# Gated attention with a routed mixture of experts: the up projections turned round, with the weights as the stationary operand

## What is computed

```python
scores = softmax(xf @ Wg.T); w, idx = top_k(scores, 2); w = w / w.sum(-1)
h1 = _lora_in(xf, W1, b1, A1, B1)      # xf @ W1.T + low-rank part + b1
h3 = _lora_in(xf, W3, b3, A3, B3)
g  = silu(h1) * h3
y_e = _lora_out(g, W2, b2, A2, B2)
y  = einsum('te,ted->td', gates, y_e)
x  = x + tanh(g_ffn[0]) * y
```

## Time and profile before

| | us |
|---|---|
| median of 2 runs | 328.74 (328.02 to 329.46) |
| the profiled execution | 328.63 |
| its span in the trace | 326.8 |
| PE busy | 300.9 (92%) |
| DVE busy | 248.6 (76%) |
| POOL busy | 210.5 (64%) |
| ACT busy | 207.0 (63%) |
| mean granted clock of PE | 0.976 of full speed |

### The profile page before, as it was taken

One profiled execution on the slowest core, in us unless ns is written; L12 is line 12 of the kernel. 1 busy time (PEld: TensorE's weight loads), 2 busy tenths in 40 slices (PEclk: granted clock), 3 DMA queues, 4 the chain that ended last, 5 costly groups with the idle time before them and its releaser, 6 DMA issues. The chain is left out here.

```text
span 326.8 us, 7436 instructions
## 1 busy us (share of the span) xinstructions
PE 300.9 (92%) x1755; PEld 231.7 (71%) x1755; DVE 248.6 (76%) x607; ACT 207.0 (63%) x486; POOL 210.5 (64%) x246
## 2 busy tenths in 40 slices
PE   8669989989999698999999999999999999999992
PEld 4548778777887555876777667677777777777761
DVE  2678879878899988787998877577777777786771
ACT  5625756656679648769657657475675575576562
POOL 2447878967986169776474756466567767676344
PEclk9979999997999969999999999999999999999998
DMA  7957998999884248676665667576553233433300
GB/s 254 391 153 217 283 256 275 279 264 261 262 235 131 67 143 274 203 213 196 154 192 149 189 157 211 132 204 203 138 135 52 49 56 59 67 48 47 50 0 0
DMA packets 30424, 54.35 MB, mean 166 GB/s; under 512 B 7232, under 2 KB 15808, under 8 KB 30112
## 3 DMA queue, kind: packets, MB, share of 16 engines
q1 hardware_dynamic: 14672, 36.10, 34.7%
q0 software_dynamic: 7488, 9.36, 16.8%
q10 hardware_dynamic: 8224, 8.42, 8.3%
HBM read 41.92 MB, written 10.65 MB: 161 GB/s over the span
## 5 line engine op out<-in xcount | busy, mean ns | idle before, releaser
L1079 POOL DMA_INDIRECT out<-ys,cols x39 | 63.5, 1629 | 54.7 <-DMA out<-ys,cols 42.2
L883 ACT ACTIVATE gh<-bank 128x512 fp32r<-128x512 f32 x39 | 23.4, 599 | 54.6 <-PE bank L648 54.4
L640 PE MATMUL bank<-WH,xh 128*128 x156 | 55.8, 439 | 0.0
L1056 POOL DMA_INDIRECT xg<-xn_rows,colg x39 | 41.2, 1056 | 20.5 <-POOL colg L1034 10.3
L992 POOL TENSOR_TENSOR WL<-stage,WH 128x512 bf16<-128x512 f32 x38 | 48.0, 1282 | 8.2 <-ACT WH L752 8.1
L640 PE MATMUL bank<-WH,xl 128*128 x156 | 49.0, 395 | 0.0
L640 PE MATMUL bank<-WL,xb 128*128 x156 | 47.2, 384 | 0.0
L752 ACT ACTIVATE WH<-stage 128x512 fp32r<-128x512 f32 x38 | 22.9, 628 | 18.2 <-DVE stage L1112 14.9
L640 PEld LDWEIGHTS bank<-WH,xl 128*128 128x128 f32 x156 | 29.2, 188 | 6.8 <-DVE xl L1495 0.4
L657 PE MATMUL bank<-WH,gh 128*128 x156 | 32.1, 327 | 1.4 <-ACT gh L883 1.4
L1499 DVE TENSOR_TENSOR gl<-bank,gh 128x512 fp32r<-128x512 f32 x39 | 26.9, 688 | 7.9 <-ACT gh L883 7.4
(11 more groups left out here) (229 smaller groups left out, 711.7 us busy)
## 6 DMA issues: line engine op xcount, KB each, us to landing
BB<-biases_in SPq DMA_DIRECT2D x16, 640.0 KB, 4.0
stage<-w_all_in SPq DMA_DIRECT2D x38, 256.0 KB, 4.5
BA<-biases_in SPq DMA_DIRECT2D x8, 640.0 KB, 4.0
WL<-w_all_in SPq DMA_DIRECT2D x10, 256.0 KB, 4.5
LS<-WH SPq DMA_DIRECT2D x45, 48.0 KB
xn_rows<-xn ACTq DMA_DIRECT2D x8, 256.0 KB, 4.7
out<-x ACTq DMA_DIRECT2D x7, 256.0 KB, 2.5
cx<-ctxT_in ACTq DMA_DIRECT2D x6, 256.0 KB, 6.1
```

The lines of the kernel that those rows point to most:

```text
L640: last = nc.tensor.matmul(dst[:, :], lhs[p][:, c * P:(c + 1) * P], W[:, bass.ds(e * (UNITS * UC) + (2 * kind + c) * UC, HID)], start=(part ...
L883: nc.scalar.activation(gh[:], pG[:, :], ACT.Copy).then_inc(s_gh, 1)
L1056: nc.gpsimd.indirect_dma_start(out=xg[q][:], out_offset=None, in_=xn2_d[0:JA * P, :] if i < NA else xn2_d, in_offset=bass.IndirectOffsetOn ...
L1079: nc.gpsimd.indirect_dma_start(out=out_rows, out_offset=bass.IndirectOffsetOnAxis(ap=cols[:, i:i + 1], axis=0), in_=ys[p][:], in_offset=No ...
```

## The change

In `up` the operands change places. Now a 128x128 block of the weights is stationary and the 128 tokens move, so `pH1` and `pH3` hold the hidden width on the partitions, in four chunks of 128 columns of tokens. A chunk takes two bfloat16 products (`WL` by `xb`) and four float32r ones (the weights' high part by `xh` and by `xl`, for two halves of the width): 24 matmuls of 128 columns for a kind where there were 6 of 512. `g` comes out as `down` wants it, so `g_transposes` and the bank `pG` go, and ACT and DVE make `gh` and `gl` from `g` in SBUF.

The stationary float32r block has a fixed address: before a tile's kind is multiplied, SP copies that kind's 1024 columns of `WH` (128 x 1024 x 4 bytes, 512 KB) inside SBUF into one of the buffers `wk` (three, later four), two copies for each tile. `xh` and `xl` lie in one tensor `xx`. b1 and b3 become columns of the partitions: eight small loads bring them in as 64 rows of 128, PE transposes them once and ACT keeps them in `b13`; DVE adds them spread over the tokens. Only b2 is still spread over the partitions (`b2`, 128 KB for each tile). ACT's `gb` moves ahead of the parts of x.

```diff
-        xh = [sb(tiles, f"xh{p}", [P, D], F32R) for p in range(2)]
-        xl = [sb(tiles, f"xl{p}", [P, D], F32R) for p in range(2)]
-        xb = [sb(tiles, f"xb{p}", [P, D], BF16) for p in range(2)]
+        xx = [sb(tiles, f"xx{p}", [P, CH, 2, P], F32R) for p in range(2)]
+        xb = [sb(tiles, f"xb{p}", [P, CH, P], BF16) for p in range(2)]
...
+        def wk_slot(n):
+            return n % 3 if n < WFOUR else (n - WFOUR + 3) % 4
...
+            def load_bias_rows():
+                sp.wait_ge(s_qT, 2 * B)
+                for e in range(E):
+                    sp.dma_start(brow[e * BCH:(e + 1) * BCH, :], biases[e, 0:2 * HID].rearrange("(c p) -> c p", p=P)
+                                 ).then_inc(s_brow, 16)
+            def load_tile(i, kind, e):
+                n = 2 * i + kind
...
+                if wk_user(n) is not None:
+                    sp.wait_ge((s_h1, s_h3)[wk_user(n) % 2], wk_user(n) // 2 + 1)
+                sp.dma_start(wk[wk_slot(n)][:].bitcast(F32), WH[:, bass.ds(e * (UNITS * UC) + 2 * kind * UC, WCOL)].bitcast(F32)
+                             ).then_inc(s_wk[wk_slot(n)], 16)
...
+            load_bias_rows()
+            for i in range(NT_SLOTS):
+                e = expert_of(i)
+                load_tile(i, 0, e)
+                if i == 1:
+                    load_weights(E - 1, 1, 1)
+                load_tile(i, 1, e)
+                if i == 0:
+                    sp.wait_ge(s_x2, B)
+                    sp.dma_start(out_rows[(B - 1) * S:B * S, 0:D].rearrange("(t p) d -> p t d", p=P), x2[:]).then_inc(s_last, 16)
+                load_scaled(i, e)
+                if i == 1:
+                    load_units(E - 1, 1, 2)
...
+            pe.wait_ge(s_brow, 16 * E)
+            nc.tensor.transpose(pT[:, 0:E * BCH], brow, ident[0:E * BCH, 0:E * BCH]).then_inc(s_bT, 1)
             attend(B, v[1])
...
                 pos_wait(pe, s_h1b if kind == 0 else s_h3b, i)
-                for part, (lhs, W, ready) in enumerate(((xh, WH, s_xh), (xl, WH, s_xl), (xb, WL, s_xb))):
-                    if kind == 0:
-                        pe.wait_ge(ready, i + 1)
+                r = wk_slot(2 * i + kind)
+                for hc in range(HC):
+                    cols = dst[:, hc * P:(hc + 1) * P]
+                    at = lambda c: bass.ds(e * (UNITS * UC) + (2 * kind + c) * UC + hc * P, P)
...
                     for c in range(CH):
-                        last = nc.tensor.matmul(dst[:, :], lhs[p][:, c * P:(c + 1) * P],
-                                                W[:, bass.ds(e * (UNITS * UC) + (2 * kind + c) * UC, HID)],
-                                                start=(part == 0 and c == 0), stop=(part == 2 and c == CH - 1))
+                        nc.tensor.matmul(cols, WL[:, at(c)], xb[p][:, c, :], start=(c == 0), stop=False)
...
+                    if hc == 0:
+                        pe.wait_ge(s_wk[r], wk_loads(2 * i + kind))
+                    for c in range(CH):
+                        for part in range(2):
+                            last = nc.tensor.matmul(cols, wk[r][:, c * HID + hc * P:c * HID + (hc + 1) * P], xx[p][:, c, part, :],
+                                                    start=False, stop=(c == CH - 1 and part == 1))
                 last.then_inc(sig, 1)
-
-            def g_transposes(i):
-                pe.wait_ge(s_g, i + 1)
-                for c in range(HC):
-                    last = nc.tensor.transpose(pG[:, c * P:(c + 1) * P], g[:, c * P:(c + 1) * P], ident[:])
-                last.then_inc(s_gT, 1)
...
             def g_high(i):
-                act.wait_ge(s_gT, i + 1)
+                act.wait_ge(s_g, i + 1)
                 pos_wait(act, s_y, i)
-                nc.scalar.activation(gh[:], pG[:, :], ACT.Copy).then_inc(s_gh, 1)
+                nc.scalar.activation(gh[:], g[:], ACT.Copy).then_inc(s_gh, 1)
```

More of the change, by code:

```diff
@@ L69 @@
 BCOL = 2 * HID + D
+BCH = 2 * HC
+WFOUR = 9
+BRING = 3
 C_TRI, C_IOTA, C_SEG = 0, P, 2 * P
@@ L181, in flamingo @@
         colg = sb(tiles, "colg", [P, NT_SLOTS], U32); cols = sb(tiles, "cols", [P, NT_SLOTS], U32)
-        eid = sb(tiles, "eid", [1, NT_SLOTS], I32); vid = sb(tiles, "vid", [1, NT_SLOTS], I32); bid = sb(tiles, "bid", [1, NT_SLOTS], I32)
+        eid = sb(tiles, "eid", [1, NT_SLOTS], I32); vid = sb(tiles, "vid", [1, NT_SLOTS], I32)
         gsel = sb(tiles, "gsel", [P, 2 + XBUF])
@@ L200, in flamingo @@
         ys = [sb(tiles, f"ys{p}", [P, D]) for p in range(2)]
[L201 to L207, removed]
+        wk = [sb(tiles, f"wk{r}", [P, WCOL], F32R) for r in range(2)]
+        gidxA = sb(tiles, "gidxA", [P, NV], I32); sidxA = sb(tiles, "sidxA", [P, NV], U32)
+        is1A = sb(tiles, "is1A", [P, NV]); is0A = sb(tiles, "is0A", [P, NV])
+        valA = sb(tiles, "valA", [P, NV])
+        b13 = sb(tiles, "b13", [P, E, BCH])
+        wk.append(sb(tiles, "wk2", [P, WCOL], F32R))
+        b2 = [sb(tiles, f"b2_{r}", [P, D]) for r in range(BRING)]
+        wk.append(sb(tiles, "wk3", [P, WCOL], F32R))
         tiles.close()
+        brow = ys[1][0:E * BCH, 0:P]
         gidxB, sidxB = cst[:, C_TRI:C_TRI + NV].bitcast(I32), cst[:, C_TRI + NV:C_TRI + 2 * NV].bitcast(U32)
@@ L234, in flamingo @@
         s_r = sem("s_r")
-        s_bb, s_ba = [sem(f"s_bb{r}") for r in range(BRING)], [sem(f"s_ba{x}") for x in range(E)]
+        s_brow, s_bT, s_b13 = sem("s_brow"), sem("s_bT"), sem("s_b13")
+        s_b2, s_wk = [sem(f"s_b2_{r}") for r in range(BRING)], [sem(f"s_wk{r}") for r in range(4)]
         s_h1b, s_h3b, s_b2g = sem("s_h1b"), sem("s_h3b"), sem("s_b2g")
@@ L291, in ls_of, with wk_loads, wk_user @@
             return kind, (s - 1) * KINDS + kind + 1
-        def bias_loads(i):
-            return 16 * BSLOT[:i + 1].count(BSLOT[i])
+        def wk_slot(n):
+            return n % 3 if n < WFOUR else (n - WFOUR + 3) % 4
+        def wk_loads(n):
+            return 16 * sum(wk_slot(m) == wk_slot(n) for m in range(n + 1))
+        def wk_user(n):
+            return max((m for m in range(n) if wk_slot(m) == wk_slot(n)), default=None)
         def settle(eng):
@@ L436, in load_biases @@
[L436 to L440, removed]
+                    sp.wait_ge(s_last, 16)
+                if i == SAFE and kind == 0:
+                    sp.wait_ge(s_wh, (E - 1) * UNITS + 4)
+                if wk_user(n) is not None:
+                    sp.wait_ge((s_h1, s_h3)[wk_user(n) % 2], wk_user(n) // 2 + 1)
@@ new lines, in load_tile, with load_scaled @@
+                sp.dma_start(wk[wk_slot(n)][:].bitcast(F32), WH[:, bass.ds(e * (UNITS * UC) + 2 * kind * UC, WCOL)].bitcast(F32)
+                             ).then_inc(s_wk[wk_slot(n)], 16)
+            def load_scaled(i, e):
+                r = i % BRING
+                if i == 0:
+                    sp.wait_ge(s_x2, B)
+                if i == 1:
+                    sp.wait_ge(s_xn2, B)
+                    sp.wait_ge(s_last, 16)
+                if i >= BRING:
+                    sp.wait_ge(s_b2g, i - BRING + 1)
+                sp.dma_start(b2[r][:], biases[bass.ds(e, 1), 2 * HID:BCOL].to_broadcast([P, D])).then_inc(s_b2[r], 16)
@@ L618, in _ @@
             keep_clock(5, WL, pS)
-            pX, pH1, pH3, pG, pY = bank[0], bank[1], bank[2], bank[3], bank[4]
+            pX, pH1, pH3, pY = bank[0], bank[1], bank[2], bank[4]
             def x_transposes(i, q):
@@ L675, in tile @@
                 up(pH1, i, p, expert(q), 0, s_h1)
-                if not first:
-                    g_transposes(i - 1)
                 if more:
@@ L869, in _ @@
             first_two(B - 2)
-            pX, pH1, pG = bank[0], bank[1], bank[3]
+            pXc = bank[0][:, 0:D].rearrange("p (c t) -> p c t", c=CH)
             def x_parts(i, p):
@@ L938, in tile @@
                 first_gate(i, q, v)
-                if not first:
-                    g_short(i - 1)
                 if i == 2:
@@ L977, in _ @@
             x_parts(0, 0)
+            act.wait_ge(s_bT, 1)
+            nc.scalar.activation(b13[:].rearrange("p e c -> p (e c)"), pT[:, 0:E * BCH], ACT.Copy).then_inc(s_b13, 1)
             deviation(B - 1)
@@ L1487, in beside_h3 @@
                     row_kinds(2, valB[:], gidxB, gofB[:], nhB[:], sidxB, is0B, is1B)
-            pX, pH1, pH3, pG, pY = bank[0], bank[1], bank[2], bank[3], bank[4]
+            pX, pH1, pH3, pY = bank[0], bank[1], bank[2], bank[4]
+            by_chunk = lambda t: t.rearrange("p (c t) -> p c t", t=P)
             def x_rest(i, p):
@@ L1520, in tile @@
                 p = q % 2
-                x = dve.value_load(bid[0:1, i:i + 1], min_val=0, max_val=E - 1) if i >= NA else 0
+                x = dve.value_load(eid[0:1, i:i + 1], min_val=0, max_val=E - 1)
                 beside_h1(i)
-                pos_wait(dve, s_g, i)
-                if i < NA:
-                    dve.wait_ge(s_bb[BSLOT[i]], bias_loads(i))
-                elif i < NA + E:
-                    dve.wait_ge(s_ba[i - NA], 16)
+                if first:
```

(6 more changed lines are left out.)

93 lines of the change are left out of this document (37 added, 56 removed).

## The result

| | before | after |
|---|---|---|
| median, us | 328.74 (2 runs) | 376.63 (2 runs, 376.61 to 376.66) |
| ratio, 95% interval | | 1.146 (1.138 to 1.154) |
| span in the trace | 326.8 | 374.8 |
| mean granted clock of PE | 0.976 | 0.980 |

A forecast was written before the change was run, and what follows sets the result against it. PE's instructions were taken to bound the tile loop. From 326.8 us, +65.5 for 39 longer tiles, -3 for waits and -0.7 at the end gave 388.6 of span, +1.8 around it: 390 us, range 375 to 418.

The forecast's parts named there:

- The bound: Tile loop: PE's instructions set a tile's cost, pitch 4.84 us late; longer PE work is paid 39 times.
- The price of a product: `up` products of 128 columns: float32r 0.115 us, bfloat16 0.075, set by block loads; a chunk 0.61.
- The sum for a tile: PE's tile: `up` 4.88 us replaces 2.76, transposes of g save 0.44; pitch 6.52, +65.5 us over 39 tiles.
- What lies around it: Early tiles' waits swallowed by longer tiles, -3 us; end of the last tile, -0.7 us.
- The copies: Weight copies inside SBUF: with other traffic 5.31 us of all DMA engines per tile, costing nothing under PE's 6.5.
- the floor under PE: Tile loop: DMA engines' busy time would limit a tile to 5.3 us should PE be quicker.
- A: `up`: float32r loads cheaper behind 128 columns, 0.085 us instead of 0.115; time 353; chance 0.07.
- B: `up`: float32r load and moving do not overlap, 0.163 us a product; +60, time 450; chance 0.07.
- C: `up`: narrow float32r products need as many passes as plain float32, 0.216 us each; +126, time 516; chance 0.11.
- D: PE's clock falls because the array moves columns for only some 60% of a tile; 455 if lasting; chance 0.08.
- E: Copies inside SBUF run at half the loads' rate: 8.6 us a tile, DMA-bound, time 472; chance 0.05.
- F: Not slower: array keeps a block for the next product using it; time 345, or about 317; chance 0.02.

## Why the prediction was right, point by point

**The bound.** Right. PE is busy for 100.00 of 100.00 us after the change and the other engines wait for it. The two runs on columns and block show that it is the float32 loads that fill most of it.

**The price of a product.** The mechanism was right, the sizes a little high. The float32r product was taken at 0.115, and its loads stand 0.111 apart. The two bfloat16 ones were taken at 0.150 and what is left of a chunk is 0.133; among themselves they cost 0.056 (a chunk of six takes 0.33 to 0.34 in the run with all products bfloat16), and the rest is the change of type, which the forecast did not have. A chunk was forecast at 0.61 and is 0.577. The 0.213 for a product of 512 columns was misread, which the sum does not feel:

```profile
250.37 0.62 PE L640 MATMUL bank<-WH,xl 128*128 x2
250.84 0.60 PE L640 MATMUL bank<-WL,xb 128*128 x2
251.28 0.60 PE L648 MATMUL bank<-ident,g 128*128 128x128 f32 x4
```

A float32r product is (250.84 - 250.37) / 2 = 0.235, a bfloat16 one 0.22. The 1.28 for h3 runs between two starts of float32r products that are both shown before their blocks can be there, the second by more; from the start of the second `xh` load to that of the second `gh` load it is 1.38.

**The sum for a tile.** 6.52 forecast, 6.29 measured: 0.28 less for the two kinds; the transposes of x take 0.24 and not 0.13, which the earlier trace rows understated because a float32r product's start is shown while it still waits for the transpose before it; `down` takes 1.45 and not 1.51. The 0.23 are 9 of the 13 us by which the forecast was high. That is the mis-sized term. Of the rest, the first product of tile 0 starts at 119.55 and not at 122.08, 2.5 us, which I can't put down to a part of the change and which is less than the spread of the first `gh` product over the runs. The stated range is a little narrower than its own terms: they add up to 372 and 422.

**What lies around it.** Right in size: the first 24 tiles have 2.9 us over the later pitch, 3.5 expected. At the end, from the last tile but one's `gb` to the last tile's `gh`, 366.02 to 367.84, it is 1.8 us where it was 2.5 (317.04 to 319.54), the forecast 0.7 less.

**The copies.** Right that they are covered, shown by leaving them out (376.5 against 376.6); PE waited 0.5 us for them in all, the start included. Their cost to the DMA engines was overstated, 0.75 x 6.28 = 4.7 us for a tile and not 5.3. But the floor under PE is not the engines' busy time, as I had written: with less work for PE and all copies the tiles lengthen through late scatters and gathers at shares of 0.84 to 0.91, to mean pitches of 5.1 to 5.5 where PE needed 4.4 to 5.0.

**The rivals.** A (0.085 for a float32r product) is out, the same block twice in a row saves nothing. B (0.163) is out. C (four passes for narrow products) is out: with 64 columns in place of 128 the loads still stand 0.111 apart. D: the clock stays at 1.00 through the loop although the array moves columns for 63% of the tile (9472 x 0.417 ns in 6.29). E: a copy of 512 KB lands after 3.6 us with others queued, and SP's queue moved 66.42 MB in 51.1% of 374.8 us, 347 GB/s with all engines, no less than the 318 of before. F: it would have needed a mean product of 0.067, and it is 2 x 2.30 / 48 = 0.096.

The Trainium skill's 81 ns for a matmul of 128 columns with its load (TensorE: Matmul & The Clock Gate, Back-to-back issue gap) fits neither kind of product here: bfloat16 ones take 56 in a row, float32r ones 111. Its rule that FP32 blocks get no fast load (Weight-path perf modes) agrees with both.

No run here gives a complete kernel faster than the one before. What the runs point to, products of 256 columns in groups, is at 326.4 us without its copies and without the additions that its two halves need, which is no gain; the copies cost its ungrouped form 12 us.

## What to carry to other kernels

Before turning a product round, count the loads and not the columns: as many columns cut into four times as many blocks cost here 2.30 us in place of 1.38 for a kind, because a float32 block loads in 0.11 us and 128 columns cover only half of that. Where float32 blocks can't be avoided, at least 256 columns should move ahead of each, and the products of the short type should stand together, not between them.

Price the prize as well as the cost. The transposes took 0.44 us of PE in each of 39 tiles, and taking them out gave 4 us and not 17, because the next limits lay just beneath: scatters and gathers, in part slowed by other DMA traffic, and waits for ACT and DVE.

## What the runs showed of the hardware that I had not expected

A block loads behind the moving of the product before it, except a bfloat16 block behind a float32r product, whose load began 0.12 after the start of that product of 256 columns and not at once. So the order of products sets the time: the same sixteen took 1.68 us in twos and 1.47 in eights. A float32 block of 64 columns loads in about half the time of one of 128 (0.053 saved of 0.111). A float32 transpose cost 0.11 wherever it stood, though its block loads in 0.06: that fits the moving of 128 columns in plain float32. Indirect transfers are late before the DMA engines are full: at a share of 0.84 to 0.90 PE's loads waited up to 3.7 us for a gather.
